# A hybrid attention kernel: values of both head halves in three split products, exponentials over pairs of banks, and new instruction lists on every engine

## The reference

```python
x = x + _L0_attn_a_ref(_layernorm(x, axis=-1), Wq, bq, Wk, bk, Wv, bv, Wo, bo)
x = x + _L0_ffn_ref(_layernorm(x, axis=-1), router_w, router_b, w1, b1, w2, b2)
x = x + _L0_attn_b_ref(_layernorm(x, axis=-1), ...)
x = x + _L0_ffn_ref(_layernorm(x, axis=-1), ...)
```

```python
scores = jnp.einsum('bhqd,bhkd->bhqk', q, k) * scale
sparsity = scores.max(axis=-1) - scores.mean(axis=-1)
_, top_idx = jax.lax.top_k(sparsity, U)
...
attn = jax.nn.softmax(scores_sel, axis=-1)
out_sel = jnp.einsum('bhuk,bhkd->bhud', attn, v)
```

## Time and profile before

| | |
|---|---|
| median of three runs | 1611.66 us (1608.55 to 1612.22) |
| profiled execution, its own time | 1608.24 us |
| span of the profiled execution, first to last instruction | 1606.5 us |
| mean granted TensorE clock | 0.976 of 2.4 GHz |
| busy share of the span | PE 93%, DVE 68%, ACT 43%, POOL 34% |
| attention part | up to about 550 us of the span |

### The profile page before, as it was taken

The page is one execution under the profiler, slowest core; times in us unless marked ns, Lnnn a source line. Parts: engine busy times, 40 slices in busy tenths (PEclk is TensorE's granted clock), DMA queues, the critical chain, the costliest instruction groups (busy, mean ns, idle before and its releaser), DMA issues.

```text
span 1606.5 us, 25861 instructions
## 1 busy us (share of the span) xinstructions
PE 1494.6 (93%) x8904; PEld 1073.0 (67%) x8904; DVE 1092.3 (68%) x2111; ACT 683.3 (43%) x1226; POOL 550.3 (34%) x696
## 2 busy tenths in 40 slices
PE   8999999999899489999989899999999999999898
PEld 7444444444443278888857687878788888878787
DVE  6877887887877946555657768577685857666532
ACT  1577777777777222222233332334333333432221
POOL 6454544545531024223220433233232323332420
PEclk9999999999999789999999999999999999999899
DMA  4323223223221210200110100101010000100001
GB/s 130 93 58 67 64 58 68 61 57 72 42 60 36 91 45 27 66 27 27 35 40 1 40 1 15 27 1 39 0 39 0 21 18 0 39 0 14 14 1 27
DMA packets 56415, 61.05 MB, mean 38 GB/s; under 512 B 15733, under 2 KB 41637, under 8 KB 56349
## 3 DMA queue, kind: packets, MB, share of 16 engines
q1 hardware_dynamic: 42653, 43.89, 10.7%
q0 software_dynamic: 13408, 16.29, 4.7%
...
...
## 4 chain that ended last, share of the span: by engine, by line
PE 51%; issue 24%; DVE 12%; POOL 8%; ACT 3%; DMA 1%; SPq 1%; POOLq 0%; ACTq 0%; DVEq 0%
PE ps L1892 13%; PE ps L1920 9%; PE ps L885 6%; PE ps L860 5%; PE ps L873 5%; POOL h L1495 3%; DVE mc L545 3%; PE ps L817 3%; POOL kT L1468 2%; PE ps L1903 2%; PE ps L829 2%; PE ps L1932 1%; DVE race L658 1%; DVE top L657 1%; PE ps L1878 1%
## 5 line engine op out<-in xcount | busy, mean ns | idle before, releaser
L545 DVE TENSOR_REDUCE mc<-ps 128x2 f32<-128x1024 f32 x256 | 305.3, 1218 | 55.1 <-PE ps L860 54.9
L1920 PE MATMUL ps<-w_hi,h 128*128 128x256 f32 x1024 | 219.0, 298 | 7.8 <-DVE h L1732 7.7
L1799 ACT ACTIVATE h<-ps 128x512 fp32r<-128x512 f32 x128 | 75.5, 598 | 309.2 <-PE ps L1950 309.1
L281 POOL DMA_DIRECT2D k_st<-k_hi x256 | 124.0, 490 | 224.3 <-PE ps L873 142.9
L1920 PEld LDWEIGHTS ps<-w_hi,h 128*128 128x128 f32 x1024 | 165.4, 188 | 14.3 <-DVE h L1732 12.3
L1892 PE MATMUL ps<-xT_b,w_hi 128*128 128x512 f32 x512 | 166.8, 407 | 0.0
L1732 DVE SCALAR_TENSOR_TENSOR h<-ps,h 128x512 fp32r<-128x512 f32 x128 | 87.4, 690 | 110.4 <-ACT h L1799 108.8
L1495 POOL TENSOR_TENSOR h<-hf,h 128x512 fp32r<-128x512 f32 x56 | 72.5, 1294 | 254.5 <-DVE h L1745 254.5
L860 PE MATMUL ps<-k_st,q_st 48*128 48x512 f32 x512 | 127.8, 495 | 21.0 <-DVE mc L545 14.3
L873 PE MATMUL ps<-q_st,k_st 64*128 64x512 f32 x512 | 138.4, 426 | 5.5 <-ACT pT0a L740 4.4
L1920 PE MATMUL ps<-w_lo,h 128*128 128x256 f32 x512 | 143.0, 279 | 0.0
...
## 6 DMA issues: line engine op xcount, KB each, us to landing
q_st<-q_hi SPq DMA_DIRECT2D x256, 32.0 KB, 2.2
k_st<-k_hi POOLq DMA_DIRECT2D x256, 32.0 KB, 1.9
q_st<-q_lo SPq DMA_DIRECT2D x128, 32.0 KB, 2.0
k_st<-k_lo POOLq DMA_DIRECT2D x128, 32.0 KB, 2.0
...
```

The source lines that it names most:

```text
L281: eng.dma_start((q_st, k_st)[which][par][64 * e + DH * r:64 * e + DH * r + DH, j, :].bitcast(F32), src[(2 * j + e) * DH:(2 * j + e + 1) * ...
L545: v.tensor_reduce(mc[par][:, qt, 2 * HU + j:MC:NPAIR], ps[:, at:at + 2, :], AX_X, ALU.max).then_inc(max_done, 1)
L1799: a.activation(h[s][m % 2][0][:, :], ps[:, RING[s] + m % 2, :], ACT.Relu).then_inc(F[s]["relu"], 1)
L1920: last = t_.matmul(ps[:, ACC[s] + t // 2, (t % 2) * D:(t % 2 + 1) * D], h[s][m % 2][a][:, t * P:(t + 1) * P], ws[k][:, m, :], start=m == 0 ...
```

## The change

- **Values.** V is done in odd units alone, for both halves of the heads at once, in two tasks V0 and V1 of two token tiles each. Each tile takes three split products of 256 columns over two chunks (`xT_hi`, `xT_lo` against the two parts of `w_v`). `values` adds the bias in two pieces for each task: the even half goes to `vz[0]`, the odd half to a new buffer `v_next`, from which POOL copies it to `vz[1]` in the even unit (`move_values`). `w_v` is split once at the start, on ACT and POOL.
- **Halved projections.** K and Q are two entries each on PE, so that other work can stand between the halves.
- **Pairs of banks.** Both T of a pair are issued together, after one wait; one exponential takes both banks, 1024 columns.
- **Lists.** The steps and `TASKS` places give way to `PE_UNITS`, `ACT_UNITS` and `DVE_UNITS`, one list for each engine and kind of unit: ("T", p, h) is the T of half h for step p + 1, ("exp", p, h) its exponential. `START`, `MERGED` and `CLOSE` are the same pieces in another order.
- `maxes`, `means` and `b1_rest` share memory.

```diff
...
-TASKS = [[("V", 0, "E"), ("X0", 0, "L"), ("X1", 1, "E"), ("K", 2, "E"), ("Q", 3, "E"), ("O1", 4, "E"),
-          ("mx", 5, "L"), ("mean", 6, "E"), ("O0", 7, "E")],
-         [("V", 0, "E"), ("K", 1, "E"), ("Q", 2, "E"), ("O1", 4, "E"), ("mx", 5, "L"), ("mean", 6, "E"),
-          ("O0", 7, "E")]]
-TASKS_FIRST = ["X0", "X1", "Q0", "K0", "mean0", "V", "Q1", "K1", "mean1", "mx"]
-FIRST_BANKS = {"X0": 7, "X1": 6, "Q0": 5, "K0": 4, "mean0": 7, "V": 5, "Q1": 7, "K1": 7, "mean1": 7, "mx": 7}
+TASKS = [["X0", "X1", "K", "Q", "O1", "mx", "mean", "O0"], ["V0", "K", "Q", "V1", "O1", "mx", "mean", "O0"]]
+TASKS_FIRST = ["X0", "X1", "Q0", "K0", "mean0", "V0", "Q1", "V1", "K1", "mean1", "mx"]
+FIRST_BANKS = {"X0": 7, "X1": 6, "Q0": 5, "K0": 4, "mean0": 7, "V0": 5, "V1": 5, "Q1": 7, "K1": 7, "mean1": 7, "mx": 7}
...
+PE_UNITS = {
...
+    "odd": [("V0",), ("T", 0, 0), ("S", 0), ("AV", 0), ("T", 0, 1), ("S", 1), ("S", 2), ("K", 0), ("T", 1, 0),
+        ("K", 1), ("S", 3), ("S", 4), ("T", 1, 1), ("AV", 1), ("S", 5), ("T", 2, 0), ("AV", 2), ("S", 6), ("T", 2, 1),
+        ("Q", 0), ("Q", 1), ("T", 3, 0), ("AV", 3), ("S", 7), ("T", 3, 1), ("V1",), ("T", 4, 0), ("S", 8), ("S", 9),
+        ("T", 4, 1), ("AV", 4), ("S", 10), ("T", 5, 0), ("S", 11), ("O1",), ("T", 5, 1), ("mx",), ("AV", 5),
+        ("T", 6, 0), ("S", 12), ("AV", 6), ("T", 6, 1), ("S", 13), ("mean",), ("T", 7, 0), ("S", 14), ("O0",),
+        ("S", 15), ("T", 7, 1), ("AV", 7)],
+    "even": [("S", 0), ("T", 0, 0), ("S", 1), ("X0",), ("S", 2), ("T", 0, 1), ("X1",), ("AV", 0), ("T", 1, 0),
+        ("AV", 1), ("S", 3), ("S", 4), ("T", 1, 1), ("K", 0), ("K", 1), ("S", 5), ("T", 2, 0), ("S", 6), ("AV", 2),
+        ("T", 2, 1), ("Q", 0), ("S", 7), ("T", 3, 0), ("Q", 1), ("S", 8), ("T", 3, 1), ("AV", 3), ("S", 9),
+        ("T", 4, 0), ("S", 10), ("AV", 4), ("T", 4, 1), ("O1",), ("S", 11), ("T", 5, 0), ("mx",), ("AV", 5),
+        ("T", 5, 1), ("S", 12), ("mean",), ("T", 6, 0), ("S", 13), ("AV", 6), ("T", 6, 1), ("O0",), ("S", 14),
+        ("T", 7, 0), ("AV", 7), ("S", 15), ("T", 7, 1)],
...
+ACT_UNITS = {
...
+    "odd": [("out", 0), ("exp", 0, 0), ("exp", 0, 1), ("exp", 1, 0), ("exp", 1, 1), ("K",), ("exp", 2, 0),
+        ("exp", 2, 1), ("Q",), ("exp", 3, 0), ("out", 1), ("exp", 3, 1), ("exp", 4, 0), ("exp", 4, 1), ("exp", 5, 0),
+        ("O1",), ("exp", 5, 1), ("mx",), ("exp", 6, 0), ("exp", 6, 1), ("mean",), ("exp", 7, 0), ("O0",),
+        ("exp", 7, 1)],
+    "even": [("out", 0), ("exp", 0, 0), ("X0",), ("exp", 0, 1), ("X1",), ("exp", 1, 0), ("exp", 1, 1), ("K",),
+        ("exp", 2, 0), ("exp", 2, 1), ("exp", 3, 0), ("Q",), ("exp", 3, 1), ("out", 1), ("exp", 4, 0), ("exp", 4, 1),
+        ("O1",), ("exp", 5, 0), ("mx",), ("exp", 5, 1), ("mean",), ("exp", 6, 0), ("exp", 6, 1), ("O0",),
+        ("exp", 7, 0), ("exp", 7, 1)],
...
+DVE_UNITS = {
...
+    "odd": [("V0",), ("max", 0), ("max", 1), ("max", 2), ("max", 3), ("max", 4), ("K",), ("stats", 0), ("stats", 1),
+        ("max", 5), ("max", 6), ("Q",), ("max", 7), ("V1",), ("max", 8), ("stats", 2), ("max", 9), ("max", 10),
+        ("max", 11), ("max", 12), ("stats", 3), ("max", 13), ("max", 14), ("max", 15), ("shares",)],
...
+    v_next = sb("v_next", [P, NT, HU, DH], F32)
...
+        eng.wait_ge(wv_ready, 1)
+        g_.tensor_tensor(w_v[1][:, :, :], stage[3], w_v[0][:, :, :].bitcast(F32), ALU.subtract).then_inc(wv_ready, 1)
...
+        def move_values(u):
+            no = free_no(u - 1, u // 2 - 1, 1, "V1") if u else free_first("V1")
+            eng.wait_ge(misc_free, no + 1)
+            if u:
+                eng.wait_ge(av_done, NGR * u)
+            g_.tensor_copy(vz[1][:, :, :, 0:DH], v_next[:, :, :, :]).then_inc(v_moved, 1)
...
-        def values(g, no):
+        def values(k, b, no):
             eng.wait_ge(task_done, no + 1)
-            src = first_bank["V"] if isinstance(no, int) and no == TASKS_FIRST.index("V") else misc
-            v.tensor_tensor(vz[g][:, :, :, 0:DH],
-                            src[:, :].rearrange("p (t h d) -> p t h d", t=NT, d=DH),
-                            bv_all[:, g * P:(g + 1) * P].rearrange("p (h d) -> p h d", d=DH).unsqueeze(
-                                1).to_broadcast([P, NT, HU, DH]), ALU.add).then_inc(misc_free, 1)
+            first = isinstance(no, int) and no < len(TASKS_FIRST)
+            src = first_bank[f"V{k}"] if first else misc
+            for g in range(2):
+                if g and not first:
+                    eng.wait_ge(v_moved, b)
+                half = slice(NT // 2 * k, NT // 2 * (k + 1))
+                last = v.tensor_tensor(vz[0][:, half, :, 0:DH] if g == 0 else v_next[:, half, :, :],
+                                       src[:, L // 2 * g:L // 2 * (g + 1)].rearrange("p (t h d) -> p t h d", h=HU, d=DH),
+                                       bv_all[:, g * P:(g + 1) * P].rearrange("p (h d) -> p h d", d=DH).unsqueeze(
+                                           1).to_broadcast([P, NT // 2, HU, DH]), ALU.add)
+            last.then_inc(misc_free, 1)
         def score_max(n, odd, par, h):
...
-            eng.wait_ge(sT_even, 2 * n + half + 1)
+            eng.wait_ge(sT_done, 2 * n + half + 1)
             if not (isinstance(u, int) and n < 2):
                 eng.wait_ge(av_done, n - 1)
             at = pair_at(u, half)
-            a.activation(pT[p % 2][half][:, 0, :], ps[:, at, :], ACT.Exp).then_inc(exp_even, 1)
-            eng.wait_ge(sT_done, 2 * n + half + 1)
-            a.activation(pT[p % 2][half][:, 1, :], ps[:, at + 1, :], ACT.Exp).then_inc(exp_done, 1)
+            a.activation(pT[p % 2][half][:, :, :], ps[:, at:at + 2, :], ACT.Exp).then_inc(exp_done, 1)
+        eng.wait_ge(stage_in[3], 16)
+        a.activation(w_v[0][:, :, :], stage[3], ACT.Copy).then_inc(wv_ready, 1)
...
-        def v_task(g, out=misc):
-            for t in range(NT):
+        def v_task(k, out=misc):
+            for t in range(NT // 2):
+                n = 0
                 for c in range(NC):
-                    last = t_.matmul(out[:, t * P:(t + 1) * P], xT[:, c, t * P:(t + 1) * P],
-                                     w_v[:, c, g * P:(g + 1) * P], start=c == 0, stop=c == NC - 1)
+                    for i, j in PASSES:
+                        at = NT // 2 * k + t
+                        last = t_.matmul(out.rearrange("p (g t n) -> p t g n", g=2, t=NT // 2)[:, t, :, :],
+                                         xT_parts[i][:, c, at * P:(at + 1) * P], w_v[j][:, c, :],
+                                         start=n == 0, stop=n == NC * len(PASSES) - 1, skip_group_check=True)
+                        n += 1
             return last
...
-        def scores_T(u, par, p, half, e):
+        def scores_T(u, par, p, half):
             n = 2 * (NGR * u + p) + half
             j, kt = 2 * (p // NT) + half, p % NT
-            if p == 0 and half == 0 and e == 0:
+            if p == 0 and half == 0:
                 eng.wait_ge(m_in, 32 * u + 32)
             if not (isinstance(n, int) and n == 0):
-                eng.wait_ge((exp_even, exp_done)[e], n - pair_ahead(u))
-            t_.matmul(bank[pair_at(u, half) + e][:, :], k_st[par][64 * e:64 * e + 64, j, kt * P:(kt + 1) * P],
-                      q_st[par][64 * e:64 * e + 64, j, :], start=True, stop=True).then_inc((sT_even, sT_done)[e], 1)
-        def products(u, g, p):
+                eng.wait_ge(exp_done, n - pair_ahead(u))
+            for e in range(2):
+                last = t_.matmul(bank[pair_at(u, half) + e][:, :], k_st[par][64 * e:64 * e + 64, j, kt * P:(kt + 1) * P],
+                                 q_st[par][64 * e:64 * e + 64, j, :], start=True, stop=True)
+            last.then_inc(sT_done, 1)
...
+            if n == EARLY[0] + 2:
+                eng.wait_ge(misc_free, 3)
+                v_task(1, first_bank["V1"]).then_inc(task_done, 1)
...
+            if c:
+                qk_half("QK".index(t), g, c).then_inc(task_done, 1)
+                return
...
-START = ["p0.mask", "init0", "p0.T", "init1", "p1.mask", "p0.wo", "p0.x", "f0.ln", "f0.T", "f0.rt", "f0.lg",
-         "f0.m0c", "p1.T", "f0.mk", "f0.m1c", "f0.m0", "p1.wo", "p1.x", "f0.m1", "f0.d0", "f0.m2", "f0.d1",
...
-         "f0.d5", "f1.rt", "wt10", "f0.m7", "f1.lg", "f0.d6", "f0.d7", "z.T", "f0.end", "z.o0", "z.o1", "wt11",
-         "z.o2", "og", "wt12", "z.o3", "z.o4", "z.o5", "z.o6", "z.o7", "z.o8", "f1.m0c", "rec0", "f1.m1c",
-         "rec1", "f1.mk", "rec2", "f1.m0", "rec3", "rec4", "f1.m1", "rec5", "z.y", "f1.d0", "f1.m2", "f1.d1",
...
+START = ["p0.mask", "p1.mask", "p0.T", "p1.T", "init0", "p0.wo", "p1.wo", "p0.x", "f0.ln", "f0.T", "f0.rt",
+         "f0.lg", "init1", "f0.m0c", "f0.mk", "f0.m1c", "f0.m0", "f0.m1", "p1.x", "f0.d0", "f1.ln", "f0.m2",
+         "wt0", "f0.d1", "f0.m3", "f1.T", "f0.d2", "f0.m4", "f1.rt", "f0.d3", "f0.m5", "f1.lg", "f0.d4",
...
+         "f0.d4", "wt10", "f0.m6", "f0.d5", "wt11", "f1.rt", "f0.m7", "f1.lg", "f1.m0c", "f0.d6", "f0.d7",
```

(65 more changed lines are left out.)

176 lines of the change are left out of this document (88 added, 88 removed), and 86 rows, old and new, of tables (CLOSE, MERGED, PE_UNITS, START).

## The result

The changed kernel takes 1624.65 us (median of 5 runs, 1621.67 to 1629.77) against 1611.66 for the kernel before. With the runs of before that went with it the ratio is 1.0084, 95% interval 1.0068 to 1.0101: slower by 0.8%, where 1583 was forecast.

The account below looks back on a forecast made before the run. PE, busy 93% of the span, was taken to set the pace. Units -20, ends of attention -2 and block lists -7 sum to -29 us, giving a forecast of 1583 us, own range 1571 to 1594, wider range 1558 to 1612.

Parts of the forecast that it names:

- the waits that a pair keeps: Attention pairs: of 4.4 us the count did not see, 1.4 go and 3.0 stay, so a pair takes 57.9.
- The count: Attention pairs: the larger of PE's list and the T loop per step, 27.1 odd plus 27.8 even, 54.9 us.
- Late Q: Rival, even units: Q stands later, its 24 transfers delay S by 1.2 us once a unit, 15.6 us: 1598; chance 0.18.
- Unit 0: Start of attention: unit 0 has no V any more, -1.98 us; V0 and V1 in the filling before it cost +1.03.
- New lists in the units: Units 1 to 13: a pair takes 57.9 us, 3.07 less than before; 6.5 pairs give -20.0 us.
- The copy of the values on POOL: Even units: POOL's new copy stands ahead of the K transfers, K is ready some 9 us in; costed at nothing.
- The end of attention: Unit 14 loses the V ahead of its maxima, 1.0 us taken; with unit 0 and the filling, -2.0 together.
- unit 15's matrix work is free there: End of attention: PE stands 15.9 us until DVE's choice is done, so only how early unit 14's maxima finish counts.
- Late T: Rival, slower: T starts late after exponentials and the loop sets the pace; half an AV late gives 1624; chance 0.14.
- The loop: From T to T, with one exponential for both banks: 1.52 us (1.45 to 1.66), against PE's mean share of 1.65.
- Values: V's 24 split products of 256 columns take 2.81 us a pair instead of 3.96, saving PE 1.15.
- Block lists: Block part: head -2.8, third stage's waits -4.0, other reorderings 0 give or take 8; together -7 us.

Follow-up runs that it names:

- best: Changed kernel with Q earlier, POOL's later-weight splits only at even units' ends, two bank pairs in the last two units, unit 0's T rows sent earlier: 1581.88 us.
- two_pairs: Changed kernel, with T halves taking turns on two pairs of banks in the last two units once unit 14's maxima are done: 1627.11 us.
- v_twice: `best` with each split product of V made twice, the second writing the same place: 1607.47 us, ratio 0.9974 to the kernel before.

## Why the prediction was wrong

- **The step that failed** is the waits that a pair keeps. The count gave 54.9 us, and the rest was taken from the old order: "How much of this stays is unknown, between 0 and 4.4"; 3.0 were put on it. The pairs take 63.7, so 8.8 are waits and slow clock: the new lists made new waits, Late Q and the held subtraction. With both taken away, in `best`, the six pairs forecast at 348.6 take 349.0, a rest of 3.3 a pair. That the guess of 3.0 comes so near is luck within its 0 to 4.4.
- **Late Q** was named as a rival and then priced from a row of before: "The longest such wait now is 1.2 us; once a unit, over 13 units, it costs 15.6: 1598." It should have been worked out from the new list: `q_lo` behind the maximum of S8, six issues of 0.61, the landing, against what PE has left before S11. That is 3.1 us in each even unit and 2.7 in unit 0, and 1.5 a later pair for the slower clock; 23 us in the medians. Alone these 23 would still have left the change faster than before, at an estimated 1606 (1583 and 23). It takes the held subtraction (10) beside it to make it slower; the rest lies at the start and the end of attention.
- **Unit 0** was to lose 1.98; the whole start is 8.1 us over the forecast. 3.7 are the rows for T, which stand behind the twelve late issues in SP's queue; I looked at S behind these issues and not at what else is queued there. 2.7 are Late Q, of which the kernel before already had 1.6: the earlier trace rows begins at 121 us and doesn't show it. T's waits for exponentials are 3.9 instead of 0.7 up to 100 us, and the granted clock is 0.50 from 92 to 98 us. In `best` 2.9 of the 8.1 are left, with a wait of 2.1 for `q_lo`.
- **New lists in the units** counted X0 and X1 by their copies on ACT. That DVE's subtraction for X1 would now fall beside POOL's split was not seen: 12.8 us in the first two pairs of the traces, 10 in the medians. (With Q early, less is left of it, 9; Late Q and the subtraction together are 33.3 in the six pairs of the traces, the change less `best`.) The copy of the values on POOL, which I did cost at nothing, shows in no wait of PE from 100 to 480 us.
- **The end of attention**: "unit 15's matrix work is free there". It was free by 15.9 us before; with the new lists, one pair of banks and T loops of 1.62 us, stretched to 1.9 and 2.6 at the lower clock, DVE waits 6.5 us for it after the choice. `two_pairs` shows the place; what it is worth in time the block part's clock hides.
- **Late T** had a chance of 0.14 and is refuted: T waits 6 us for exponentials in 380. The loop I put at 1.52 (1.45 to 1.66) is 1.62, the exponential at 1.06 is 1.02.
- **Values**: twelve products take 1.44 us, 2.88 a pair (forecast 2.81). That a microsecond saved on PE is most of one in time, `v_twice` shows from the other side (2.5 for 2.88).
- **Block lists**: -7 forecast; -6.4 between the profiled executions of before and of the change, -6.8 in the medians. The 3.06 us for `w_g` are gone, the head waits 3.3 instead of 5.4. Since block parts with the same lists differ by up to 8.6 us in the traces, so near a hit is luck in part.

Against the forecast, cut by cut: 8.1 (start) + 33.7 (pairs, 33.3 of it by the experiments) + 1.9 (units 13 and 14) + 5.9 (end of attention) + 0.6 (block) = 50.2, and from the forecast's 1577.6 (the sum of its cuts) to the span of 1627.7 there are 50.1. What the 1.9 are was not tried, and of the 5.9 some 5 go with the clock of that execution.
